# Part of the causal mask in unused contraction rows, half of the key layout on VectorE, the second norm on ScalarE

## The reference

```python
x = x + tanh(g_xattn[0]) * xattn(layernorm(x), ctx, ctx, W, b, mask)   # causal: key k only for token t >= k
x = x + tanh(g_ffn[0]) * ffn(layernorm(x), ...)
# xattn: softmax(where(masked, -inf, q @ k.T / 4)) @ v @ W.T + b
# ffn: a shared swiglu MLP for all tokens, plus h * weight @ w2[e].T for the two chosen of 8 experts
```

## Time and profile before

| | |
|---|---|
| median of 3 runs | 1125.04 us (1122.34 to 1125.54) |
| the profiled execution: time | 1116.76 us |
| its span | 1115.0 us |
| mean granted TensorE clock | 0.99 |
| TensorE busy | 1066.6 us, 96% |
| VectorE busy | 835.2 us, 75% |
| GpSimd busy | 520.2 us, 47% |
| ScalarE busy | 472.6 us, 42% |

### The profile page before, as it was taken

One profiled execution on the slowest core, in us unless ns is written; L12 is line 12 of the kernel. 1 busy time (PEld: TensorE's weight loads), 2 busy tenths in 40 slices (PEclk: granted clock), 3 DMA queues, 4 the chain that ended last, 5 costly groups with the idle time before them and its releaser, 6 DMA issues.

```text
span 1115.0 us, 22178 instructions
## 1 busy us (share of the span) xinstructions
PE 1066.6 (96%) x7283; PEld 897.8 (81%) x7283; DVE 835.2 (75%) x1859; ACT 472.6 (42%) x722; POOL 520.2 (47%) x617
## 2 busy tenths in 40 slices
PE   5779999999999999999999999999998999999997
PEld 3557888788788888888887778888887888888886
DVE  6677886987987888878868765466443788888886
ACT  4566656555565666566565432233221111111110
POOL 6434447456465465474483333000002566666564
PEclk9899999999999999999999999999999999999999
DMA  7888856666765767576465113787553555554451
GB/s 144 179 173 129 201 136 120 149 131 146 122 152 126 119 142 141 122 143 156 111 96 135 31 38 127 241 261 225 183 171 116 161 164 153 164 158 155 151 169 64
DMA packets 108130, 161.84 MB, mean 145 GB/s; under 512 B 29101, under 2 KB 72943, under 8 KB 108017
## 3 DMA queue, kind: packets, MB, share of 16 engines
q1 hardware_dynamic: 96244, 122.40, 47.2%
q0 software_dynamic: 11776, 38.03, 11.3%
HBM read 76.43 MB, written 52.12 MB: 115 GB/s over the span
## 4 chain that ended last, share of the span: by engine, by line
PE 84%; DVE 9%; issue 3%; ACT 2%; POOL 1%; DMA 0%; POOLq 0%; ACTq 0%; DVEq 0%
PE ps L781 16%; PE ps L726 13%; PE ps L828 13%; PE ps L743 7%; PE ps L830 6%; PE ps L648 4%; PE ps L636 4%; PE ps L679 3%; PE ps L813 3%; PE ps L601 3%; PE ps L657 2%; DVE mneg L1230 2%; PE ps L631 2%; PE ps L607 1%; PE ps L702 1%
## 5 line engine op out<-in xcount | busy, mean ns | idle before, releaser
L828 PE MATMUL ps<-regr,gh 128*128 x600 | 221.5, 407 | 0.1
L905 ACT ACTIVATE Pt<-ps,pbias 77x1024 f32<-77x1024 f32 x128 | 141.5, 1106 | 89.8 <-PE ps L636 86.3
L830 PE MATMUL ps<-regr,gl 128*128 x600 | 169.9, 283 | 0.0
L828 PEld LDWEIGHTS ps<-regr,gh 128*128 128x128 f32 x600 | 113.8, 190 | 23.8 <-issue 0.5
L995 ACT ACTIVATE gh<-ps 128x512 fp32r<-128x512 f32 x75 | 44.8, 599 | 204.8 <-PE ps L813 204.8
L1420 POOL TENSOR_TENSOR gl<-gf,gh 128x512 fp32r<-128x512 f32 x64 | 82.5, 1291 | 99.2 <-ACT gh L867 98.9
L1230 DVE TENSOR_REDUCE mneg<-ps 128x8 f32<-128x616 f32 x128 | 100.3, 792 | 22.6 <-PE ps L601 15.8
L830 PEld LDWEIGHTS ps<-regr,gl 128*128 128x128 f32 x600 | 114.0, 190 | 0.0
L726 PE MATMUL ps<-x2h,winh 128*128 128x512 f32 x256 | 108.1, 422 | 0.6 <-DVE OHR L1110 0.6
L726 PE MATMUL ps<-x2h,winl 128*128 128x512 f32 x256 | 101.0, 394 | 0.0
L726 PE MATMUL ps<-x2l,winh 128*128 128x512 f32 x256 | 100.8, 394 | 0.0
(11 more groups left out here) (208 smaller groups left out, 2655.2 us busy)
## 6 DMA issues: line engine op xcount, KB each, us to landing
regr<-regr SPq DMA_DIRECT2D x96, 256.0 KB, 5.9
y_dram<-Pt SPq DMA_DIRECT2D x64, 256.0 KB, 2.1
regf<-in_x SPq DMA_DIRECT2D x32, 256.0 KB, 2.9
x<-in_x SPq DMA_DIRECT2D x32, 256.0 KB, 4.3
y_dram<-res SPq DMA_DIRECT2D x32, 256.0 KB, 2.4
regr<-regr SPq DMA_DIRECT2D x96, 77.0 KB, 6.8
x_dram<-x2h SPq DMA_DIRECT2D x14, 512.0 KB, 3.0
x_dram<-x2l SPq DMA_DIRECT2D x14, 512.0 KB, 3.8
```

The source lines that it names most:

```text
L828: e.matmul(o, gh2[:, k % 3, fc, :], w2v[:, bass.ds(val, 1), fc, :, :].rearrange("p o h d -> p (o h) d"), start=fc == 0, stop=False, skip_g ...
L830: m = e.matmul(o[:, 0, :], gl2[:, k % 3, fc, :], w2v[:, bass.ds(val, 1), fc, 0, :].rearrange("p o d -> p (o d)"), start=False, stop=fc == ...
L905: e.activation(Pt[0:K, 4 * k:4 * k + 4, :].rearrange("k (n j) t -> k n (j t)", n=2), bank_of["sc", b, k][0:K, :, :], ACT.Exp, bias=pbias[: ...
```

## The change

The products of maxima and scores have rows of the contraction that carry nothing. The change puts part of the mask there.

- **Maxima.** `xTh` for this use is replaced by `xM[q]`: for q = 0 the data stand in rows 0 to 63 and a unit matrix for tokens 0 to 63 in rows 64 to 127; for q = 1 the other way round. `Kbd`'s zero rows hold `caus` for keys of those tokens. So tokens 0 to 63 are masked in the product itself; the separate mask covers keys 65 to 76 only, 4 x 12 = 48 columns rather than 308, and is added behind the product (as before). ScalarE makes `xM` with two copies of 64 partitions ahead of `xTh`; `xM`, `xTh` and `xTl` have one buffer each, `xTh` and `xTl` had two.
- **Scores.** The contraction has 128 rows rather than 100: rows 100 to 127 hold a unit matrix for tokens 0 to 27 in `Xs` and the mask values in `Kst`, both written once. The separate mask covers tokens 28 to 76: 98 columns rather than 154.
- **Keys.** Each layout operation is now 64 partitions x 616; GpSimd makes rows 0 to 63, VectorE rows 64 to 127 (stage `keys`, k = 1, slot 3).
- **Second norm.** ScalarE makes it (scale and bias by pointer), in the same place of the list (slot 7, behind the last exp and ahead of the tanh of the slot); GpSimd's `root` computes the bias with two more small operations.
- At the start: two fills of `Kbd`'s mask rows on ScalarE, a memset and two copies for `xM` on VectorE, two memsets of `Xs` rows on GpSimd; the memset of `Vau` moves to a later slot.

```diff
-KR = 100
+KR = 128
+TOK = 28
+LATE = 64
+        def keys(e, b, j):
+            rows, m = slice(64 * j, 64 * j + 64), slice(4 * j, 4 * j + 4)
+            return e.tensor_tensor(Kbd[rows, b % G, :, m, :],
+                                   khi[rows, b % G * 2:b % G * 2 + 2, :].bitcast(F).unsqueeze(2).broadcast_to([64, 2, 4, K]),
+                                   own8[rows, m].unsqueeze(1).unsqueeze(3).broadcast_to([64, 2, 4, K]), ALU.mult)
...
# TensorE, max
-                        m = e.matmul(o[:, q], xTh[:, h, c, t * P:(t + 1) * P], Kbd[:, g, c, 4 * q:4 * q + 4, :], start=True, stop=t == 1)
+                        m = e.matmul(o[:, q], xM[:, q, c, t * P:(t + 1) * P], Kbd[:, g, c, 4 * q:4 * q + 4, :], start=True, stop=t == 1,
+                                     skip_group_check=True)
-                            m = e.matmul(o[:, q], identb[:, :], caus[:, :].unsqueeze(1).broadcast_to([P, 4, K]), start=False, stop=True)
+                            m = e.matmul(o[:, q, :, LATE + 1:K], identb[:, :],
+                                         caus[:, LATE + 1:K].unsqueeze(1).broadcast_to([P, 4, K - LATE - 1]), start=False, stop=True,
+                                         skip_group_check=True)
# TensorE, scores
-                        e.matmul(pair[0:K, n, :].rearrange("k (j t) -> k j t", j=2)[:, :, 0:K], identb[0:K, 0:K],
-                                 cauT[:, :].unsqueeze(1).broadcast_to([K, 2, K]), start=True, stop=False, skip_group_check=True)
+                        e.matmul(pair[0:K, n, :].rearrange("k (j t) -> k j t", j=2)[:, :, TOK:K], identb[0:K, 0:K],
+                                 cauT[:, TOK:K].unsqueeze(1).broadcast_to([K, 2, K - TOK]), start=True, stop=False, skip_group_check=True)
# ScalarE, xT
-                    if b >= 2:
-                        e.wait_ge(s[f"xs{h}"], 48 * (b // 2))
-                        e.wait_ge(s["mm"], 4 * (b - 1))
-                    e.activation(xTh[:, h, :, :], bank_of["xT", b, 0][:, :].rearrange("p (c t) -> p c t", c=2),
-                                 ACT.Copy).then_inc(s["xTh"], 1)
+                    if b == 0:
+                        e.wait_ge(s["dcon"], DCON["rows"])
+                    else:
+                        e.wait_ge(s["mm"], 4 * b)
+                    v = bank_of["xT", b, 0][:, :].rearrange("p (c t) -> p c t", c=2)
+                    for j in range(2):
+                        i = e.activation(xM[64 * j:64 * j + 64, j, :, :], v[64 * j:64 * j + 64], ACT.Copy)
+                    i.then_inc(s["xTh"], 1)
+                    if b >= 1:
+                        e.wait_ge(s[f"xs{1 - h}"], 48 * ((b + 1) // 2))
+                    e.activation(xTh[:, :, :], v, ACT.Copy).then_inc(s["xTh"], 1)
# ScalarE, new
+                elif stage_ == "norm2":
+                    if b >= 1:
+                        e.wait_ge(s["x2T"], b)
+                    e.wait_ge(s["nm2"], 4 * b + 4)
+                    for t in range(2):
+                        i = e.activation(xn2[:, t, :], x1[:, b % NX, t, :], ACT.Identity, bias=nm[:, 1, t:t + 1],
+                                         scale=rs[:, 1, t:t + 1])
+                    i.then_inc(s["n2"], 1)
# VectorE
+                elif stage_ == "keys" and k == 1:
+                    e.wait_ge(s["khi"], b // G + 1)
+                    if b >= 2:
+                        e.wait_ge(s["mm"], 4 * (b - 1))
+                    keys(e, b, 1).then_inc(s["klo"], 1)
-                elif stage_ == "norm2":
...
-                        i = e.tensor_scalar(xn2[:, t, :], x1[:, b % NX, t, :], mv[:, 1, t, 0:1], rs[:, 1, t:t + 1],
-                                            ALU.subtract, ALU.mult)
# GpSimd
-                elif stage_ == "keys":
+                elif stage_ == "keys" and k == 0:
...
-                    e.tensor_tensor(Kbd[:, b % G, k, :, :], khi[:, b % G * 2 + k, :].bitcast(F).unsqueeze(1).broadcast_to([P, 8, K]),
-                                    own8[:, :].unsqueeze(2).broadcast_to([P, 8, K]), ALU.mult).then_inc(s["kbd"], 1)
+                    keys(e, b, 0).then_inc(s["kbd"], 1)
# GpSimd, root(n, b), now for both norms
+                e.tensor_tensor(mr[:, n, :], mv[:, n, :, 0], rs[:, n, :], ALU.mult).then_inc(done, 1)
+                e.wait_ge(done, 4 * b + 3)
+                e.tensor_scalar(nm[:, n, :], mr[:, n, :], -1.0, None, ALU.mult).then_inc(done, 1)
```

More of the change, by code:

```diff
@@ L38 @@
 DCON = {n: i + 1 for i, n in enumerate(
-    "idb m8 tgh brow pbias crow kcol ones rec pre_zero pre wgh0 lb0".split())}
-GCON = {n: i + 6 for i, n in enumerate("ident caus cauT upb kint ramp ks0 va_zero va_one ks1".split())}
+    "idb m8 rows tgh brow pbias crow kcol ones rec pre_zero pre wgh0 lb0".split())}
+GCON = {n: i + 6 for i, n in enumerate("ident caus cauT upb kint ramp ks0 xs0 va_zero va_one xs1 ks1".split())}
 ROUTES = [(4 * c - 4, 8, c) for c in range(1, NCH - 2, 2)] + [(4 * c, 4, c) for c in (NCH - 2, NCH - 1)]
@@ L118, in phase_one @@
             slots[2] += [("khi", 0, 0), ("klo", 0, 0), ("kv", 0, 0)]
-            slots[8].append(("vau", 0, 0))
-            slots[9] += [("table", 0, 0), ("own", 0, 0)]
+            slots[9] += [("table", 0, 0), ("own", 0, 0), ("vau", 0, 0)]
         if i == 1:
@@ L303, in build @@
         Kbd = carve(P, [G, 2, 8, K])
-        xTh = carve(P, [2, 2, S])
-        xTl = carve(P, [2, 2, S])
+        xTh = carve(P, [2, S])
+        xTl = carve(P, [2, S])
+        xM = carve(P, [2, 2, S])
         w1_at = used[0]
@@ L883, in scalar @@
                         i = e.activation(xn[:, t, :].rearrange("p (c r q) -> p c q r", c=2, q=4),
-                                         xt[:, h, t, :].rearrange("p (c q r) -> p c q r", c=2, q=4), ACT.Identity, bias=mr[:, 1, t:t + 1],
+                                         xt[:, h, t, :].rearrange("p (c q r) -> p c q r", c=2, q=4), ACT.Identity, bias=nm[:, 0, t:t + 1],
                                          scale=rs[:, 0, t:t + 1])
@@ L1155, in vector @@
             e.tensor_reduce(own8[:, :], ident[:, :].rearrange("p (j d q) -> p j q d", j=2, q=4), AX, ALU.add).then_inc(s["dcon"], 1)
+            e.memset(xM[:, :, :, :].bitcast(F), 0.0).then_inc(s["lo"], 1)
+            e.wait_ge(s["lo"], 1)
+            for j in range(2):
+                rows = slice(64 - 64 * j, 128 - 64 * j)
+                i = e.tensor_copy(xM[rows, j, :, 0:LATE], ident[rows, rows].unsqueeze(1).broadcast_to([64, 2, LATE]))
+            i.then_inc(s["dcon"], 1)
             routing = None
@@ L1222, in vector @@
                 elif stage_ == "xT":
-                    e.wait_ge(s["xTh"], b + 1)
-                    low(xTl[:, h, :, :], ("xT", b, 0), xTh[:, h, :, :]).then_inc(s["xTl"], 1)
+                    e.wait_ge(s["xTh"], 2 * b + 2)
+                    low(xTl[:, :, :], ("xT", b, 0), xTh[:, :, :]).then_inc(s["xTl"], 1)
                 elif stage_ == "max":
@@ L1452, in gpsimd @@
                 if stage_ == "norm" and b == 0:
+                    e.wait_ge(s["nm"], 4)
+                    e.memset(Xs[96:KR, 0, :, :, :].bitcast(F), 0.0).then_inc(s["gcon"], 1)
+                    e.wait_ge(s["gcon"], GCON["xs0"])
+                elif stage_ == "table":
                     e.memset(Vau[:, :, :, :, :], 0.0).then_inc(s["gcon"], 1)
@@ L1581 @@
         _np.diff([p_[0] for p_ in pairs]), _np.diff([p_[1] for p_ in pairs])]).astype(_np.float32)
-    own = _np.zeros((4, 2, H, K), _np.float32)
+    own = _np.zeros((32, 2, K), _np.float32)
     for r_ in range(4):
         own[r_, r_ % 2] = 1.0
-    arrays["own"] = own.reshape(4, -1)
+    for r_ in range(TOK):
+        own[4 + r_, :, r_ + 1:] = NEGS
+    arrays["own"] = own
     nc = _bacc.Bacc("TRN2", target_bir_lowering=False, num_devices=1)
```

87 lines of the change are left out of this document (47 added, 40 removed), and 2 rows, old and new, of the table names.

## The result

The changed kernel takes 1157.05 us (1155.23 to 1158.5), the kernel before beside it 1123.81: 1.0293 times, interval 1.0279 to 1.0308. It is slower, as forecast, by 33 us where 14.4 were forecast; 1157 lies 3 us above the range.

A forecast was written before the change was run, and what follows sets the result against it. TensorE was taken to bound the steady stretch, a latency chain the start. Masks -9.1, ScalarE +18.5 and start +5 sum to +14.4 us on the 1125.04 us reference: 1139.4 us forecast, range 1127 to 1154.

The forecast's parts named there:

- Masks, -9.1: TensorE, steady stretch: shorter masks gain 0.35 per iteration (first pair 0.02, second 0.23, scores 0.10), 26 times: 9.1 us gained.
- Rival D: TensorE masks: weight loads set the pace, only 6 us gained, 1142 us; forecast together with D 63%.
- ScalarE, +18.5: Steady stretch: xM copies and norm2 ahead of L912 make TensorE's L614 later by 1.26, 1.01 or 0.3: 18.5 us lost.
- GpSimd, 0: Two more small operations ahead of norm2: scaling factor still ready in time, cost 0, bounds 0 and 0.5.
- VectorE's layout, 0: VectorE loses the second norm, gains a 616-element layout where it was idle: 0, bounds -0.1 and +0.3 per iteration.
- SyncE's single buffer, 0: Input spreads need the single xTh buffer free; issued half an iteration early, so 0; uncovered, each would hold ScalarE.
- The start, +5: First inputs, chain through L892: xM copies add 0.98 five times, 4.9; taken as +5 us, bounds 2 and 8.
- The end, 0: End of the attention phase: VectorE relieved, last norm takes longer: 0, bounds -2 and +2.
- A: Rival, faster: wait at L614 does not grow, added ScalarE work finds room elsewhere; about 1118 us, 10%.
- B: Rival, break-even: all terms in their best corner, norm2 as cheap as a plain copy; 1127 us, 12%.
- C: Rival, delay compounds: norm2 costs 0.62, exp late for the values' second half, VectorE's layout holds the maxima; 1158 us, 15%.
- What would show it: Signs: L614 waits for L912 26 times, over 25 us; TensorE about 95 of 100; norm2 0.8 from tanh; first scores wait longer.

The follow-up runs named there:

- c1: Changed kernel with norm2 back on VectorE, xM copied from xTh in SBUF at slot 10, two buffers for xTh and xTl: 1116.09 us, 0.9993 times before.
- b1: Kernel before with the second norm alone moved to ScalarE, its bias on GpSimd: 1143.42 us, 1.0175 times before.
- b2: Kernel before with only two 64 x 512 copies from PSUM added ahead of xTh, into a tile nobody reads: 1135.93 us, 1.0107 times before.
- a1: Changed kernel with the second norm back on VectorE, all else kept, plus GpSimd's wait for its key layout: 1132.27 us, 1.0069 times before.
- a4: Changed kernel with xM copied from xTh in SBUF at slot 10, norm2 still in slot 7, plus GpSimd's wait: 1146.42 us, 1.0202 times before.
- a0: Control: changed kernel with one more wait, GpSimd waiting for its own key layout: 1155.92 us, 1.0286 times before.
- d1: Same kernel as a0, run again on a chip of the second kind (before takes 1115 to 1116 there): 1157.24 us, 1.0376 times before.
- a3: Changed kernel with two buffers for xTh and xTl, as before the change, plus GpSimd's wait: 1154.11 us, 1.0276 times before.
- c3: c1 with VectorE's late-row copies behind the first moments and, in the first two inputs, xM copies ahead of the own-rows copy: 1109.67 us, 0.9952 times before.
- e2: c3 run again, on another chip of the second kind: 1110.61 us, 0.9943 times before.
- b3: Kernel before with the scores' mask rows alone (28 rows in the products, separate mask 98 columns): 1121.71 us, 0.9982 times before.
- e1: b3 run again on a chip of the second kind: 1115.11 us, 0.9990 times before.

## Why the prediction was right or wrong

**The account of the steady stretch** closes. From before to c1: 489.67 to 479.64, that is busy time -12.3 (the masks) and idle +2.3. From c1 to after: 479.64 to 512.64, +33.0, of which idle is 25.7 (20.9 before L633, 4.4 more before L617) and busy time 7.3. Of the 7.3, some 1.7 are the clock (below), and 5.8 the products of the values: by the distances between their starts, 800 of L665 take 47.5 in c1 and 53.3 in after. The parts taken alone do not quite make the whole: b1 21.2, b2 8.3 (without its 4.3) and the masks' -10.0 make 19.5, after has 23.0; a1 should be 8.3 - 10.0 = -1.7 and has 2.0. By these differences the copies cost some 3 to 4 us more beside the shorter masks than without them; why was not followed.

**Forecast and measurement, place by place.** Against the recorded profile 14.4 were forecast and 40.3 measured. Steady stretch: 9.4 forecast, 23.0 measured. Start: 5 and 11.5. End: 0 and 6.0. So about half of the miss is the steady stretch, and there it is the term of ScalarE.

**Masks, -9.1: right.** Measured -10.0. The late masks' starts are 6.5 us apart in sum, waits left out, where they were 16.9: 0.21 a pair against the 0.23 taken. The scores' went from 9.8 to 7.7, 0.021 a pair against 0.025. Rival D is out. One step was too gloomy: the first pair was to give 0.02 and gave 0.12. The first scores do wait for VectorE's copy of the attention output, as the earlier trace rows had it, and the sum of these waits grows from 1.9 to 4.1 us; but they wait 12 times of 25 in c1, where it was 18 times in before, so less than half of the 0.21 is given back. With 0.12, 0.21 and 0.08 an input the 25 inputs make 10.3. The rule of the Trainium skill that was weighed here ("TensorE: Matmul & The Clock Gate", section "LDWEIGHTS (loading the stationary operand)") gives 64 ns for the load of 77 columns, and taken as a floor of the pace it would have made the gain 0.01. The rows do not agree with it as a floor: in c1 the second mask of a pair starts 50 ns behind the first and the product 27 ns behind the second, each with a load of its own.

**ScalarE, +18.5: the mechanism right, the size wrong; this is the step that failed.** The forecast's sum was L614 later by 1.26, 1.01 and 0.3. In its place the runs show L633 later by 25.8 us in sum, and two losses beside it, 4.4 and 1.7. Less the 8.4 that the masks give outside the stretch up to L633 (c1 gains only 1.6 of its 10.0 in it), that is 23.5, where the stretch lost 23.0.
- The prices. The xM copies take 0.61 each, not 0.49, and a norm2 0.49, not 0.40. L633, measured from the first transpose, stands 1.57 later in seven inputs with tanh, 1.30 in six, and 0.53 to 0.64 in those without: 7 x 1.57 + 6 x 1.30 + 12 x 0.58 = 25.8 where the forecast's like sum was 18.5. The row for the copies was there and was passed over: the earlier trace rows has L892 handing over after 0.62. I took the shortest hand-over of a kind (tanh to gh) instead of the one of this very copy.
- The values, taken as no stall. The margin was said to be 0.1 to 0.2; exp came 0.25 later than planned, and the second half of the values ran at its pace, 0.13 to 0.28 longer in an input than in c1 or 5.8 us in all. a4, where xM is out of the way, has 48.3 instead of 53.3 for these products, a1, where only norm2 is, has 52.9: it is the copies ahead of exp. But this stall is no loss of its own in after: L633 comes behind these products and waits for L939 in all 25 inputs, 0.3 to 1.3 each. Without the stall it would have waited that much longer. The 5.8 are inside the 25.8, not beside them.
- Two terms that no step had: the clock, told below, 1.7, and the 4.4 us before L617, where VectorE's L1099 takes 1.85 beside GpSimd's layout and addition. The latter are gone in a0, d1 and a3 (0.9), which all carry GpSimd's extra wait, and which have two or three falls of the clock more and about the same steady loss (23.0 to 24.6).

**norm2 on ScalarE for norm2 on VectorE.** It was priced at 0.40 per half, between 0.31 and 0.62, and 0.49 was measured against 0.62 for the strided norm with the same pointers. The rule of the Trainium skill on lines of 16 bytes ("SBUF — State Buffer", section "Door 1: The DMA port swizzle"), weighed beside it, points the same way: the two kinds of operation last 0.59 and 0.83, both read 256 columns and two pointers, and they differ in the stride of what they write. But its price is not its duration. Taken out of the changed kernel it gives back 22.1 of the steady stretch (24.1 in a0 to 2.0), put into before it costs 21.2: 16.1 are idle before L615 and 6.8 the clock, less than 2 us of this hidden again.

**GpSimd, 0: right in the changed kernel's steady stretch, and only there.** No idle stands before L952 in after, and one of 0.7 in a0, d1 and a3 each. a4 and b1 show the cover gone: 1.1 to 1.8 in six of the 13 inputs with tanh and 0.3 to 0.6 in six more.

**VectorE's layout, 0: right.** c1 has it, and its steady stretch is 10.0 shorter. What VectorE loses in after, the 4.4 at L1099, it loses beside GpSimd's work, and c1 has it not.

**SyncE's single buffer, 0: wrong at the start.** The sentence on the lost cover was the mechanism. The chain of after's start:

```profile
16.84 6.98 DMA regr<-regr
...
23.85 0.61 ACT regr L920
...
44.32 9.06 DMA regr<-regr
...
53.89 1.11 ACT Pt L932
```

The xTh copy, with exp behind it, waits for the spreads of the input before, which lie on SyncE's queue behind the key spreads. Two buffers give 2 to 3 us (a3's start of 8.2 against 10.4 in a0 and 11.2 in d1).

**The start, +5: too small by half.** 10.4 to 11.5 were measured in a0, d1 and after. Its parts, as far as they are shown: 6.3 are the pairs of xM copies (b2 has them alone; 1.2 a pair instead of 0.98), 2 to 3 the single buffer, and 1.4 the row copies on VectorE, which were in the diff and were counted among "added memsets", though they stand on the chain ahead of the first moments. That makes about 10 to 11. The first of the row copies takes 1.39 and ends just when GpSimd's memset (2.78 to 4.92) has ended:

```profile
3.61 1.40 DVE regr L1200
```

In c3 the same two copies, begun at 4.67, take 0.60 together. c3's gain over c1, 8.3 to 2.5 (3.3 in e2), is only in part one of the changed kernel's own losses: in c1 the xM copies came behind the 2.26 us copy of the own rows, and VectorE got the first maxima at 16.67, against 15.07 in after and 12.68 before.

**The end, 0: wrong, +6.0.** The last norm2 waits for GpSimd, whose queue is full of scatters; the chain:

```profile
646.22 0.97 POOL tab_dram L1562
...
648.66 0.25 POOL nm L1477
...
649.50 0.58 ACT xn L952
650.08 0.48 ACT tt L981
650.56 0.52 ACT gh L884
651.08 0.49 ACT regf L939
...
651.62 0.39 PE ps L633
```

Where norm2 is back on VectorE (a1, c1) 2.4 are left, where it is alone on ScalarE (b1) 5.5.

**The reference point.** "The median of the runs is 8.3 above that execution" was taken for a constant. It was the difference of two kinds of runs, most likely of chips, and the changed kernel takes the same on both. Made against one chip of the second kind, the forecast of +14.4 stands against +42.2; on the first kind, against +33.2.

**Rivals.** A and B are out. C named the time, 1158, but by luck: of its three causes norm2 at 0.62 and VectorE's layout holding the maxima did not happen (VectorE did hold them, by L1099), and the third, exp late for the values, happened and cost nothing of its own. **What would show it**: L633 waiting for L939 26 times over 25 us (d1: 40.8 us, 27 times, before the weight load), TensorE near 95 of 100 (94.72 from 200 to 300 us) and norm2 0.8 ahead of tanh (0.98) were all met in kind. The first scores, which "should wait longer", do: 4.0 us in after where it was 1.9.

## What to carry to other kernels

Ask of an operation that is moved to a half idle engine what is queued behind it there, and add the delay of each thing that follows, with the hand-over times of those very operations, not of the cheapest of their kind. A queue that is idle 40% of the time had 0.28 us of room at the place that counted; xM's copies, four slots further on and with norm2 back on VectorE (c1), cost nothing in the steady stretch. And when an operation is moved, list the answers it waits for from other queues: norm2 alone on ScalarE cost twice what was expected, since its bias came late. A control run is read in its profile too, not only in its time: here it took away one loss of 4.4 us and brought another.

## What the runs showed of the hardware

**The clock falls behind long waits of TensorE.** In d1, windows of TensorE's granted clock (the number third from the end), and the product that ended an idle of 1.30:

```profile
231.00:235.00 4.00, 4.00 (x24) 3.20 (x23) 3.90 (x11) 2.93 (x5) 1.30 (x4) 1.00 1.03 259
235.00:240.00 5.00, 3.67 (x38) 2.18 (x38) 3.59 (x8) 4.29 (x8) 1.34 (x2) 0.85 0.00 0
240.00:245.00 5.00, 5.00 (x29) 4.13 (x29) 3.14 (x11) 1.01 (x2) 1.35 (x4) 0.81 0.70 110
245.00:250.00 5.00, 5.00 (x43) 4.18 (x42) 4.70 (x8) 3.20 (x6) 3.76 (x3) 1.00 0.47 55
...
238.48 0.61 PE L633 MATMUL ps<-ident,regr 128*32 128x128 f32 x2 [1.30 <-ACT regf L939]
```

A mean between 1.00 and 0.5 is time shared between 2.4 and 1.2 GHz. One such fall costs about 1.7 us (5 x 0.15 + 5 x 0.19, what the clock lacks in the two rows). The steady stretch has one in after, four in d1, a0 and b1, three in a3, two in a4, each within about a microsecond of an idle of TensorE of 1.3 to 2.4. It has none in the other runs, where no idle of TensorE is above 0.8. It does not follow every such idle: 1 of 13 in after, 4 of 13 in d1. So a stall above a microsecond costs more than itself, and not the same in every run.

**One kernel differs by 7 to 9 us in 1116 from chip to chip, another does not.** On the first kind ScalarE stands idle 1.6 to 2.0 us before a values copy, six times in b3's steady stretch, and for five of them the profile names no engine as the releaser ("remote"); on the second kind (e1) the same inputs have 0.27 there, none is "remote", and 1121.71 becomes 1115.11. What ScalarE waits for there is not settled: the profile does not show it, and no run told it apart, nor the chip from the hour.

**A copy on 64 partitions is not cheaper than one on 128**: 0.59 for each L916, 0.60 for L920.

**Some VectorE operations take longer beside GpSimd's, others do not.** L1099 takes 1.85 in after, begun during GpSimd's key layout and ended 0.29 behind the addition that follows, and 0.61 otherwise; the first row copy takes 1.39 beside a memset of GpSimd and 0.34 in c3, begun when that memset is nearly done. The statistics L1037 of c3, at 3.61 in the middle of the same memset, take 0.75 for two, no longer than elsewhere (0.74 at 11.13). What decides it was not tested.
